# Two attention stages: the causal mask moves from TensorE to VectorE, the score products are regrouped, and the copies of keys and queries are sent later

## The reference, cut to what matters

```python
scores = einsum('bqhd,bkhd->bhqk', qq, kk) * scale      # 16 heads, 512 x 512
scores = where(causal, scores, finfo.min)               # the plain attention: MASK_BIAS
probs = softmax(scores, axis=-1)
y = einsum('bhqk,bkhd->bqhd', probs, v) @ W_o
```

## Time and profile before

| what | value |
|---|---|
| median of 3 runs | 3233.5 us (3221.18 to 3238.54) |
| the profiled execution | 3232.98 us |
| its span, first to last instruction | 3231.2 us |
| mean granted clock of TensorE | 0.919 |
| TensorE busy in the span | 2618.4 us, 81% |
| VectorE busy | 2178.6 us, 67% |
| ScalarE busy | 1414.6 us, 44% |
| GpSimd busy | 1177.9 us, 36% |

### The profile page before, as it was taken

How to read it: one execution, slowest core, us unless ns; L and a number is a source line. 1 busy time by engine, 2 the same in 40 slices (tenths; PEclk the granted TensorE clock), 3 DMA queues, 4 the chain that set the end, 5 groups by cost and what they waited for, 6 DMA issues and landing times. The chain is left out here.

```text
span 3231.2 us, 51537 instructions
## 1 busy us (share of the span) xinstructions
PE 2618.4 (81%) x17479; PEld 2011.4 (62%) x17479; DVE 2178.6 (67%) x5628; ACT 1414.6 (44%) x2412; POOL 1177.9 (36%) x2298
## 2 busy tenths in 40 slices
PE   1445873999999999948888759999999997698972
PEld 1423662777777777636666647777777766486861
DVE  5733773777777767448888846676767754677785
ACT  0001330455555555511111225666666652586861
POOL 3210110334434344322222113454455442773076
PEclk9997995899999999969999969999999995799996
DMA  2144001213223222031110032222122114697772
GB/s 29 32 134 127 23 13 30 41 29 44 42 29 47 37 34 41 15 104 50 49 49 32 3 43 33 31 40 36 25 40 40 26 17 165 231 296 225 250 218 73
DMA packets 198657, 228.02 MB, mean 71 GB/s; under 512 B 48621, under 2 KB 148814, under 8 KB 190478
## 3 DMA queue, kind: packets, MB, share of 16 engines
q1 hardware_dynamic: 188302, 207.69, 26.7%
q0 software_dynamic: 8192, 16.79, 1.6%
q10 hardware_dynamic: 2048, 2.10, 0.2%
HBM read 132.55 MB, written 58.10 MB: 59 GB/s over the span
## 5 line engine op out<-in xcount | busy, mean ns | idle before, releaser
L1394 PE MATMUL banks<-Kb,Qb 96*128 96x128 f32 (+3 forms) x2048 | 599.6, 348 | 58.6 <-issue 27.3
L1406 PE MATMUL banks<-Qb,Kb 98*128 98x512 f32 (+3 forms) x2048 | 602.7, 356 | 4.8 <-ACT mha_prob L1297 1.0
L1101 DVE TENSOR_REDUCE mha_nm<-banks 128x1 f32<-128x384 f32 (+3 forms) x704 | 421.5, 639 | 185.9 <-PE banks L1398 172.3
L1101 DVE TENSOR_REDUCE mla_nm<-banks 128x1 f32<-128x384 f32 (+3 forms) x704 | 419.9, 638 | 160.0 <-PE banks L1398 146.5
L1297 ACT ACTIVATE mla_prob<-banks 128x512 f32<-128x512 f32 x640 | 376.5, 598 | 311.6 <-PE banks L1406 303.2
L1394 PEld LDWEIGHTS banks<-Kb,Qb 96*128 96x128 f32 x2048 | 364.3, 195 | 216.5 <-issue 159.9
L1297 ACT ACTIVATE mha_prob<-banks 128x512 f32<-128x512 f32 x640 | 375.7, 598 | 273.7 <-PE banks L1406 260.8
L1216 POOL TENSOR_SCALAR_AFFINE_SELECT mla_prob<-mla_prob 128x256 f32<-128x256 f32 (+1 forms) x640 | 237.8, 379 | 405.3 <-PE banks L1394 379.7
L1406 PEld LDWEIGHTS banks<-Qb,Kb 98*128 98x128 f32 x2048 | 334.8, 193 | 47.1 <-issue 7.6
L1216 POOL TENSOR_SCALAR_AFFINE_SELECT mha_prob<-mha_prob 128x256 f32<-128x256 f32 (+1 forms) x640 | 225.6, 361 | 355.4 <-PE banks L1394 329.2
L1828 PE MATMUL banks<-glu_wd,glu_hid 128*128 128x128 f32 x1024 | 147.7, 288 | 74.3 <-DVE glu_hid L1707 74.1
(11 more groups left out here) (434 smaller groups left out, 5392.1 us busy)
## 6 DMA issues: line engine op xcount, KB each, us to landing
moe_wt<-expert_rows SPq DMA_DIRECT2D x53, 1024.0 KB
conv_tz<-conv_kernel SPq DMA_DIRECT2D x16, 1024.0 KB, 6.8
moe_xg<-slots SPq DMA_DIRECT2D x53, 256.0 KB
results<-moe_yt SPq DMA_DIRECT2D x53, 256.0 KB
Kb<-mla_kh SPq DMA_DIRECT2D x32, 256.0 KB, 4.9
Qb<-mla_qh SPq DMA_DIRECT2D x128, 64.0 KB
Kb<-mha_kh SPq DMA_DIRECT2D x32, 256.0 KB, 5.6
Qb<-mha_qh SPq DMA_DIRECT2D x128, 64.0 KB
```

The costliest lines, as they stand in the source:

```text
L1101: dve.tensor_reduce(nm[:, g % 2, h:h + heads, j], ps[:, bank1(g, k), 0:heads * w].rearrange("p (h k) -> p h k", h=heads), axis=AX.X, op=AL ...
L1394: one = pe.matmul(ps[:, bank, x * w:(x + 1) * w], Qb[0:MROW, u, g, h + x, j * P:(j + 1) * P], Kb[0:MROW, u, g, 0:w], start=(x == 0), stop= ...
L1406: last = pe.matmul(ps[:, S2 + k % 2, at:at + w], Kb[0:MROW + 2, u, grp, kb * P:(kb + 1) * P], Qb[0:MROW + 2, u, grp, h, kb * P:L], start=T ...
```

## The change

The mask products, the `identr` tile and the three-dimensional mask go. The mask is a [128, 512] tile, zero but for its last 128 columns. VectorE adds its last w columns to the w scores and reduces in one instruction. `UNITS1` becomes 12 units: four of 512 columns, four of 384 + 128, four of 256.

```diff
-UNITS1 = [(0, 0, HG)] + [(1, h, 2) for h in (0, 2)] + [(j, h, 1) for j in (2, 3) for h in range(HG)]
-UNITS2 = [u for a in (0, 2) for u in ([(a, 0, 0, L)], [(a, 3, 0, P), (a, 1, P, L - P)], ...
+UNITS = 3 * HG
+ROWS = [[(3, 0, L)], [(2, 0, 3 * P), (0, 3 * P, P)], [(1, 0, 2 * P)]]
+UNITS2 = [(0, h, 1) for h in range(HG)] + [(1, h, 1) for h in range(HG)] + [(2, 0, 2), (2, 2, 2), (3, 0, 4)]
-                                dve.tensor_reduce(nm[:, g % 2, h:h + heads, j],
-                                                  ps[:, bank1(g, k), 0:heads * w].rearrange("p (h k) -> p h k", h=heads),
-                                                  axis=AX.X, op=ALU.max, negate=True).then_inc(s1_free, 1)
+                def row_maxima(g, k):
+                    h = k % HG
+                    dve.wait_ge(s1_ready, c.next(s1_ready))
+                    for j, at, w in ROWS[k // HG]:
+                        last = dve.tensor_tensor_reduce(junk[:, k % 3, at:at + w], ps[:, bank1(k), at:at + w], mask[:, L - w:L], -1.0,
+                                                        BIG, ALU.add, ALU.min, nm[:, g % 2, h, j:j + 1])
+                    last.then_inc(s1_free, 1)
```

The scores less the maximum are made by one product a unit, over several heads where the key block is short; `e_seen`, which releases GpSimd's zeroing, is raised before the product:

```diff
                     pe.wait_ge(s2_free, c.next(s2_free))
-                    for h, kb, at, w in UNITS2[k]:
-                        last = pe.matmul(ps[:, S2 + k % 2, at:at + w],
-                                         Kb[0:MROW + 2, u, grp, kb * P:(kb + 1) * P],
-                                         Qb[0:MROW + 2, u, grp, h, kb * P:L], start=True, stop=True)
+                    pe.sem_inc(e_seen, 1)
+                    pe.matmul(ps[:, bank2(g, k), 0:WIDE[k]].rearrange("p (x w) -> p x w", x=heads),
+                              Kb[0:MROW + 2, u, grp, kb * P:(kb + 1) * P],
+                              Qb[0:MROW + 2, u, grp, h:h + heads, kb * P:L], start=True, stop=True).then_inc(s2_ready, 1)
```

The sum of the rotation and both low parts move from VectorE to GpSimd, which gets a second tile `tmpq` for the queries. SyncE sends the maxima of each group ahead of all else, and keys and queries behind them in group 2:

```diff
                     for g in range(NG):
+                        if has_maxima(turn, g):
+                            ...
+                            sp.wait_ge(ml_ready, c.next(ml_ready))
+                            sp.dma_start(f32(Qb[MROW:MROW + 2, to, grp, :, :]), ...
                         if g == 2 and turn != "last":
                             sp.wait_ge(kb_used, c.next(kb_used))
                             if proj:
                                 keys(1 - u)
-                        if has_maxima(turn, g):
-                            ...
-                        if g == 2 and turn != "last" and proj:
-                            queries(1 - u)
+                                queries(1 - u)
```

The tables of places are new (latent stage first, direct stage second); projections are cut in parts so that they fall in different units, the gather moves from unit 4 to 3, and the values are taken in three calls instead of two:

```diff
-        WIDE = 4
-        LATENTS = dict(pe=6, act=7, dve=8)
-        KEYS = dict(pe=0, turn=2, act=5, low=6) if latent else dict(pe=0, act=2, low=4)
-        QUERIES = dict(pe=6, turn=8, act=10, low=1) if latent else dict(pe=6, act=8, low=9)
-        OUT, SPLIT = 9, 7
+        GATHER, VALUES_AT, OUT, SPLIT = 3, {5: (0,), 8: (1,), 10: (2, 3)}, 11, 9
+        LATENTS = dict(pe=((0, 7), (0, 8)), act=(0, 9), dve=(0, 10))
+            KEYS = dict(pe=((1, 0), (1, 6)), turn=(1, 7), add=(1, 8), act=(1, 10), low=(2, 0))
+            QUERIES = dict(pe=((1, 9), (1, 11)), turn=(2, 0), add=(2, 2), act=(2, 3), low=(2, 5))
+            KEYS = dict(pe=((1, 0),), act=(1, 2), low=(1, 4))
+            QUERIES = dict(pe=((2, 1),), act=(2, 3), low=(2, 5))
```

More of the change, by code:

```diff
@@ L27 @@
 NEG = -1e30
+BIG = 3e38
 KPAD = P - 1
 KROW = KPAD + L + 1
-MROW = 3 * 8 * HG
+MROW = 3 * HG * HD
 CLEAR = 4 * L
@@ L943, in slots @@
                     for g in range(NG):
-                        if g == 2 and turn != "last":
-                            sp.wait_ge(kb_used, c.next(kb_used))
-                            if proj:
-                                keys(1 - u)
                         if has_maxima(turn, g):
@@ L953, in slots @@
                                          f32(mhl[:, par, :])).then_inc(m_rows[par], 16)
-                        if g == 2 and turn != "last" and proj:
-                            queries(1 - u)
+                        if g == 2 and turn != "last":
+                            sp.wait_ge(kb_used, c.next(kb_used))
+                            if proj:
+                                keys(1 - u)
+                                queries(1 - u)
                         if g == 1 and dense and latent:
@@ L970, in _ @@
                 link(dve.memset(ps[:, OB, :], 0.0))
+                link(dve.memset(mask[:, 0:L - P], 0.0))
                 if latent:
@@ L1335, in _, with three @@
                 pe.sem_inc(s2_free, 2)
-                def three(o, hi, lo, a, first=True, last=True):
+                def three(o, hi, lo, first=True, last=True):
                     pe.matmul(o, hi, xth[:, :], start=first, stop=False)
@@ L1364, in project, with queries @@
-                    if g == 2:
+                            three(ps[:, MA, :], kxh[:, 0, :], kxl[:, 0, :], first=False)
+                        else:
+                            three(ps[:, MA, :], wph[:, 0, :], wpl[:, 0, :]).then_inc(k_ready, 1)
+                    else:
+                        pe.wait_ge(mb_free, c.next(mb_free))
+                        three(ps[:, MB, :], kxh[:, 1, :], kxl[:, 1, :]).then_inc(k_ready, 1)
+                def queries(part):
+                    if part == 0:
@@ L1386, in scores @@
-                def scores(g, u, k, seen):
-                    j, h, heads = UNITS1[k]
-                    w = P * (j + 1)
-                    bank = bank1(g, k)
-                    back = 1 if g == 0 and k < 2 else 0
-                    pe.wait_ge(s1_free, c.next(s1_free) + back)
-                    for x in range(heads):
-                        one = pe.matmul(ps[:, bank, x * w:(x + 1) * w], Qb[0:MROW, u, g, h + x, j * P:(j + 1) * P],
-                                        Kb[0:MROW, u, g, 0:w], start=(x == 0), stop=False, skip_group_check=True)
-                        if seen and x == 0:
-                            one.then_inc(e_seen, 1)
-                    pe.matmul(ps[:, bank, 0:heads * w].rearrange("p (x w) -> p x w", x=heads)[:, :, w - P:w],
-                              identr[:, :], mask[:, 0:heads, :], start=False, stop=True,
-                              skip_group_check=True).then_inc(s1_ready, 1)
@@ new lines, in new_values @@
+                def new_values():
+                    pe.wait_ge(ma_free, c.next(ma_free))
+                    for b in range(BLK):
+                        tok = slice(b * P, (b + 1) * P)
+                        o = ps[:, MA, tok]
+                        if latent:
+                            last = pe.matmul(o, lats[:, 1, tok], up[:, 3, :], start=True, stop=True)
+                        else:
+                            pe.matmul(o, xth[:, tok], wph[:, 1, :], start=True, stop=False)
+                            pe.matmul(o, xth[:, tok], wpl[:, 1, :], start=False, stop=False)
+                            last = pe.matmul(o, xtl[:, tok], wph[:, 1, :], start=False, stop=True)
+                    last.then_inc(v_ready, 1)
@@ L1462, in values @@
+                def values(u, g, kbs):
+                    pe.wait_ge(p_ready, c.next(p_ready, sum(kb in kbs for kb, _, _ in UNITS2)))
+                    for kb in kbs:
                         last = times_v((g + 1) % NG, u if g == 3 else 1 - u, (g + 1) % 2, kb)
-                    if half:
+                    if BLK - 1 in kbs:
                         last.then_inc(o_ready, 1)
@@ new lines, in slots @@
+                            if dense and at == DENSE["pe"]:
+                                context_taken()
+                                output_product()
+                            if proj and latent and at in LATENTS["pe"]:
+                                latents(1 - LATENTS["pe"].index(at))
+                            if proj and at in KEYS["pe"]:
+                                keys(KEYS["pe"].index(at))
+                            if proj and at in QUERIES["pe"]:
+                                queries(QUERIES["pe"].index(at))
@@ L1502, in _ @@
                 pe.drain().then_inc(xs_taken, 1)
-                for g in range(NG):
-                    project(g, 0)
+                if latent:
+                    latents(1)
+                    latents(0)
+                for part in range(len(KEYS["pe"])):
+                    keys(part)
+                for part in range(len(QUERIES["pe"])):
+                    queries(part)
+                new_values()
                 transpose_x()
```

353 lines of the change are left out of this document (165 added, 188 removed).

## The result

The changed kernel takes 3352.5 us (3348.3 to 3358.4, 4 runs) against 3234.4 for the one before: ratio 1.0374, 95% interval 1.0339 to 1.0408, 118 us slower. The profiled execution's span is 3356.7 us, 125.5 above the span before. The forecast was 3330 us, 98 above.

What follows compares the result with a forecast made beforehand. TensorE's column time was taken to bound both attention stages; late copies and the clock add 4.0 and 2.4 us a sequence over fourteen each, 90 us, edges +8: 98 more, 3330 us (own range 3275 to 3400; stated range 3070 to 3420).

Steps and rivals of the forecast that it cites:

- The keys leave 5.3 and 6.5 us late: SyncE's queue, group 2: with maxima sent first, keys leave 5.3 (second stage) and some 6.5 us (first) after group start.
- 20.5 us from the keys to the next sequence: Both attention stages: from the keys' first copy to the next sequence's first product takes 20.5 us, whatever TensorE does.
- A wait of 5 to 6 us: Ahead of each sequence's group 0: TensorE idle 5 to 6 us for copies; groups 2 and 3 +2.0 and +3.8 us.
- The clock costs 3.7 us: Behind each sequence's wait: TensorE's granted clock falls to half, costing 3.7 us a sequence.
- Rival B: Clock behind the waits: it holds or its loss is covered, 104 us less, 3227 us, or 3279 with half; chance 0.13.
- Groups 0 and 1: -3.3 + 3.7: Each sequence's first two groups: 3.3 us saved, 3.7 lost to the clock; +0.4 second stage, +0.9 first.
- 1.65 us less in a group: TensorE, each attention group: mask products removed, scores merged, 1.65 us less a group, 6.6 a sequence.
- VectorE: +0.14 us an operation, no bound: VectorE's maxima: 0.07 us queued fixed part plus 0.07 for the reduced value, 8.4 us a group with gather; engines level.
- rival D: VectorE's maxima: VectorE becomes the bound; half rate near 3550 us, or 3375 if only the reduced value costs 150 ns; chance 0.16.
- Rival C: Start of group 0: copies are hidden, so the change is a clear gain, 180 us less, 3053 us; chance 0.21.
- Rival E: TensorE's merged score products: merging doesn't shorten its time, 3375 us; no own chance, counted within the forecast's 0.50.
- Edges +8: Stage edges: GpSimd ahead of stages +4, first sequences' later copies +10, last sequences -3 each; +8 us in all.

Runs made afterwards that it cites:

- Run 4: The kernel before, with only SyncE's order in group 2 changed to maxima, keys, queries: ratio 1.0757 to the kernel before, +253 us.
- run 2: The changed kernel with the queries' projection, turn and split back in slot 1 (first stage's keys moved ahead for room), maxima still copied first: ratio 1.0398 to the kernel before.
- run 1: The changed kernel with SyncE's old order in group 2, keys ahead of the maxima, then queries: ratio 1.0113 to the kernel before, +41 us.
- run 11: The changed kernel with 8 of the 12 query copies from the third sequence on, low part not copied: ratio 0.9982 to the kernel before, -5 us.
- run 7: The changed kernel with TensorE multiplying constants while it waits for the copies: ratio 1.0130 to the kernel before, +46 us.
- Run 10: The kernel before without the 11 mask products of a group, nothing merged, causal mask left out ahead of the maxima: ratio 1.0045 to the kernel before, +16 us.
- run 5: The changed kernel with keys copied ahead of the maxima and, in the second stage only, queries projected in slot 1: ratio 0.9922 to the kernel before, -22 us.
- run 6: As run 5, with the 16 masked maxima of a group replaced by plain reduces without the mask: ratio 0.9853 to the kernel before, -49 us.
- run 9: As run 5, with the next input's preparation and the first stage's keys one to two units earlier: ratio 0.9914 to the kernel before, -32 us.

## Why the prediction was right, and where it was off

- **TensorE is the bound; the change's waits decide.** Right: 97 to 98% busy before, 88 to 89% after, 150 us of new waits.
- **The keys leave 5.3 and 6.5 us late.** Right: 5.8 and 6.3. Run 4 shows that this order alone makes the kernel before 253 us slower.
- **20.5 us from the keys to the next sequence.** Right to the tenth (20.4, 20.5; 20.6 to 20.9 in runs 2 and 4). The margin was read 0.5 us too large: the next sequence starts at 2035.05 in the trace, and not at the 2035.6 that the prediction worked out from a mean. What the prediction missed: the queries, now projected in slot 2, are late by themselves, 9.8 us into the group, and bound the sequence at 24.3 us. It changed nothing in this kernel, but run 1 shows it. The sentence that puts the reason into the copies is right (run 11: 3.4 us for four of them).
- **A wait of 5 to 6 us.** Right: 5.1 and 5.3. Groups 2 and 3 with it took 26.2 and 26.8 us against 25.8 and 27.0.
- **The clock costs 3.7 us.** Right: 3.1 and 3.5 a sequence by run 7, and 3.9 and 3.7 in groups 0 and 1 alone. It is a mean: in single sequences of the second stage it is 1.7 to 6.2 us. Rival B is out.
- **Groups 0 and 1: -3.3 + 3.7.** This is the term that was mis-sized. At full clock they save 1.2 us, not 3.3 (22.7 against 23.95 us in the second stage, 25.05 against 26.2 in the first). With the clock's loss they were 2.6 us longer than before in both stages, where the forecast had +0.4 and +0.9. The step behind it is "1.65 us less in a group": summed from the starts of single products, it gave 6.6 us a sequence; product time fell by 3.9 (46.70 to 42.77), and of that only part is time, as new short waits came. Run 10 says the same of the mask products alone: 4.0 us a sequence forecast, some 2.2 found at full clock. What keeps TensorE from going faster in those groups I haven't settled; VectorE's reduced value is only 0.2 us of it (runs 5 and 6).
- **VectorE: +0.14 us an operation, no bound.** The reduced value cost less than assumed: the read lies under the next maximum. Half rate (rival D) is out by 689 against 685 ns; one source lies in PSUM here, which is not the case that the Trainium skill (Vector Engine (DVE) Microarchitecture Reference, "Points that are easy to get wrong") warns of.
- **Rival C, 180 us faster once the copies are hidden.** Its condition was made in run 5 in the second stage, its price fails: 22 us faster, with 2.0 us a sequence there. The same mis-sized saving.
- **Rival E, merging doesn't shorten.** Its 3375 us was as near to the result as the forecast's 3330, but merging was not tested by itself. Beside run 10, which has the mask products gone and nothing merged, the full-clock rows point both ways: groups 0 and 1 take 22.1 us there and 22.7 in run 7, groups 2 and 3 take 22.7 to 23.5 there and 20.7 to 22.3 in run 5. It stays open.
- **Edges +8.** They were -14: each stage's last interval was 7 us shorter, not 3, and the first context copy came 6 us earlier, while the way from the first stage to the second took 6 us more. The 7 us were mostly a clock of 0.98 instead of 0.77, which no term of the prediction had.

By terms: 28 sequences at 5.0 us, +140, less 14 at the edges, 125.5 against the forecast 98. The sequences were underrated by 50 us (90 forecast) and the edges overrated by 22. Since the two partly cancel, the forecast's nearness to the result is in part luck; its mechanism is not.

## What to carry to other kernels

When an edit moves a step in an in-order copy queue, measure from its issue to the one who waits, for every transfer behind it, and compare each sum with the time that the faster compute now leaves: a margin of 3 us was overrun by copies that left 6 us later. A saving on the engine that bounds a kernel can be worth nothing until the short waits it uncovers are seen to (run 10): look at the granted clock of the stage before and after, and try filling the wait with idle products before reshaping the kernel. And price removed products by a pair of whole groups at the same granted clock, from first product to first product, not by the distances of single starts.

## What the runs showed of the hardware that I had not expected

- Waits of 1.0 to 1.5 us were often followed by stretches at 0.5 (runs 9 and 10), while the kernel before kept 1.00 in its second stage with waits of 0.8 us. The length of the wait alone doesn't decide: in the steady sequences of its first stage the kernel before waits 0.26 and some 0.56 us at each group 2, and behind two of these places (1123.20 and 1177.70) the clock was 0.50 for some 10 us, behind the others not. The penalty can outweigh the work removed.
- The queries' copies move at half the DMA engines' share: 0.54 and 62 GB/s while they run alone (below), with 64 KB each, over 8 partitions of `Qb`; the stretch in which the keys' copies, over 32 partitions, are under way with queries behind them reaches 0.89.

```profile
2139.00:2143.00 4.00, 4.00 (x34) 3.47 (x27) 2.71 (x9) 2.60 (x6) 3.70 (x11) 1.00 0.89 106
2143.00:2147.00 4.00, 4.00 (x31) 2.94 (x31) 3.20 (x18) 2.28 (x5) 2.30 (x8) 1.00 0.54 62
```

- The Trainium skill (DMA: Bandwidth & Descriptors, "Why a DMA increments its semaphore by 16 and not by 1") has a rule that would explain it: a copy is spread over the largest number of engines, up to 16, that divides the outermost dimension of both sides, here 8 of 16. The shares of 0.54 and 0.89 agree; no run here reshapes the copies, so it is not shown.
- Maxima issued on ScalarE's queue landed no earlier than behind the keys on SyncE's (1.67 against 1.61 us of wait), and later once queries ran ahead.
